# Second attention: values of two pairs of heads at once from high and low parts, and weights split inside the first attention

## What is computed

```python
q = jnp.einsum('bsm,hmd->bshd', x, W_Q) + b_Q
k = jnp.einsum('bsm,hmd->bshd', x, W_K) + b_K
v = jnp.einsum('bsm,hmd->bshd', x, W_V) + b_V
scores = jnp.einsum('bqhd,bkhd->bhqk', q, k) / jnp.sqrt(jnp.float32(D_HEAD))
scores = jnp.where(causal, scores, jnp.float32(-jnp.inf))
pattern = jax.nn.softmax(scores, axis=-1)
z = jnp.einsum('bhqk,bkhd->bqhd', pattern, v)
attn_out = jnp.einsum('bqhd,hdm->bqm', z, W_O) + b_O
```

## Time and profile before

| what | value |
|---|---|
| median of 3 runs | 1392.21 us |
| the profiled execution | 1392.85 us, of which 1390.9 us from first to last instruction |
| mean granted TensorE clock | 0.986 |
| second attention | from 539 us to the end |
| one pair there (10 groups) | 102.3 to 103.3 us for pairs 1 to 6 |

### The profile page before, as it was taken

The page is one execution under the profiler, slowest core; times in us unless marked ns, Lnnn a source line. Parts: engine busy times, 40 slices in busy tenths (PEclk is TensorE's granted clock), DMA queues, the critical chain, the costliest instruction groups (busy, mean ns, idle before and its releaser), DMA issues. The chain is left out here.

```text
span 1390.9 us, 26533 instructions
## 1 busy us (share of the span) xinstructions
PE 1304.0 (94%) x9904; PEld 688.7 (50%) x9904; DVE 1027.2 (74%) x1819; ACT 753.9 (54%) x1254; POOL 684.5 (49%) x525
## 2 busy tenths in 40 slices
PE   5889999999999987989999999999999999999897
PEld 3763222222222245555655655555555655655554
DVE  7767888888888865876766766776766776766768
ACT  5476777877777874334444444444444444443343
POOL 4101150100001010658788787777788788788671
PEclk9899999999999999999999999999999999999998
DMA  1522400000000000000000000000000000000000
GB/s 36 179 101 80 133 20 1 2 1 1 1 1 1 2 1 1 1 1 1 1 1 1 2 0 2 1 1 2 1 1 1 1 1 1 1 1 1 8 9 16
DMA packets 18172, 21.58 MB, mean 16 GB/s; under 512 B 7784, under 2 KB 15872, under 8 KB 16512
## 3 DMA queue, kind: packets, MB, share of 16 engines
q1 hardware_dynamic: 18048, 19.88, 4.4%
HBM read 14.63 MB, written 5.24 MB: 14 GB/s over the span
## 5 line engine op out<-in xcount | busy, mean ns | idle before, releaser
L1751 POOL TENSOR_TENSOR acc<-acc,prob 128x1024 f32<-128x1024 f32 (+3 forms) x250 | 493.4, 1974 | 86.4 <-ACT prob L1945 51.0
L2008 DVE TENSOR_REDUCE part_max<-psum 128x1 f32<-128x512 f32 (+3 forms) x640 | 353.9, 604 | 148.4 <-PE psum L1789 75.5
L1945 ACT ACTIVATE prob<-psum 128x1024 f32<-128x1024 f32 (+3 forms) x274 | 242.9, 897 | 287.4 <-PE psum L1840 279.5
L679 DVE TENSOR_SCALAR w<-psum 128x512 f32<-128x512 f32 x472 | 304.6, 686 | 59.3 <-PE psum L536 47.6
L630 ACT ACTIVATE w<-psum 128x512 f32<-128x512 f32 x552 | 293.9, 601 | 85.9 <-PE psum L536 85.6
L556 PE MATMUL psum<-w,v_cols 128*32 128x512 f32 x2048 | 273.7, 607 | 0.0
L1859 PE MATMUL psum<-prob,v_pair 128*64 128x512 f32 (+3 forms) x1280 | 250.2, 532 | 0.6 <-POOL prob L1719 0.6
L1837 PE MATMUL psum<-q_hi,k_hi 64*128 64x512 f32 (+3 forms) x640 | 135.5, 408 | 29.0 <-DVE part_max L2008 13.5
L1859 PEld LDWEIGHTS psum<-prob,v_pair 128*64 128x64 f32 x1280 | 87.6, 137 | 144.9 <-issue 133.8
L1784 PE MATMUL psum<-k_hi,q_hi 64*128 64x512 f32 (+3 forms) x640 | 135.5, 411 | 5.7 <-DVE part_max L2008 2.4
L1837 PE MATMUL psum<-q_lo,k_hi 64*128 64x512 f32 (+3 forms) x640 | 123.5, 366 | 0.0
(11 more groups left out here) (305 smaller groups left out, 1455.8 us busy)
## 6 DMA issues: line engine op xcount, KB each, us to landing
q_rows<-q_dram SPq DMA_DIRECT2D x12, 256.0 KB
k_rows<-k_dram SPq DMA_DIRECT2D x3, 1024.0 KB
x<-in_L_attn_x SPq DMA_DIRECT2D x4, 256.0 KB, 4.0
mask<-in_L_ffn_attention_mask SPq DMA_DIRECT2D x1, 1024.0 KB, 6.4
q_dram<-x_high SPq DMA_DIRECT2D x1, 1024.0 KB, 6.8
q_dram<-x_low SPq DMA_DIRECT2D x1, 1024.0 KB, 7.1
k_dram<-q_rows SPq DMA_DIRECT2D x1, 1024.0 KB, 9.3
k_dram<-k_rows SPq DMA_DIRECT2D x1, 1024.0 KB, 6.2
```

The lines of the kernel that those rows point to most:

```text
L679: nc.vector.tensor_scalar(w[:, s % WR, 2 * m + 1, :], pair_bank[n % RING][1], 0.0, None, ALU.max)\
L1751: nc.gpsimd.tensor_tensor(sums, sums, prob[:, s % PR, :, q0:C], ALU.add).then_inc(summed, 1)
L1945: last = nc.scalar.activation(prob[:, s % PR, :, q0:C], sh.psum[:, first:first + 2, q0:C], ACT.Exp, scale=SCALE)
L2008: free(nc.vector.tensor_reduce(part_max[:, m, i, c:c + 1], src[m][:, 0:cols], AX_X, ALU.max), unit, m)
```

## The change

Five things change.

1. A value unit now serves two pairs. It makes, for four tiles of 128 tokens, three float32r products of 256 columns each into half a bank, and takes two banks. `wv_high` and `wv_low`, the parts of W_V, are made at the start of the second attention by ACT and POOL.
2. The value units are no longer in every pair. Even pairs have one in groups 0 and 1 (the last two chunks of tokens for that pair and the next), odd pairs have one in groups 7 and 8 (the first two chunks for the next two pairs). Groups 6 and 8 of even pairs, and groups 0, 1 and 6 of odd pairs, have none. Within a group the value unit now comes ahead of mix and turn. Pair 0 keeps all four at its start.
3. ACT copies each value unit in two copies of one bank, to both pairs' tiles.
4. `w_high` and `w_low` of W_K and W_Q are no longer made in `between` (one cast on ACT, one subtraction on DVE) but in the first attention: 32 casts of 128x64 on ACT, one to a step in turns 9 to 11, and two subtractions of 128x1024 on POOL behind its last chunk.
5. The bias of the values is read by TensorE as a broadcast operand, without a copy in `prob`, and ACT does not wait for that product.

```diff
@@ -471,6 +472,8 @@
         SPARE = [s for s in range(STEPS)
                  if s % T == DIVIDE and s >= T or s in AFTER and AFTER[s][1] in DVE_FULL or s < G * T and s % T == 12]
         ON_ACT = [2 * s + 1 for s in SPARE]
+        PIECES = 2 * H
+        PIECE_AT = [s for s in range(9 * T, 12 * T) if s not in SPARE and s % T not in (LAG - 1, LAG, DIVIDE - 1)][:PIECES]
         ACTS, DVES = [], []
         for n in range(2 * STEPS):
             ACTS.append((ACTS[-1] if n else 0) + (2 if n in ON_ACT else 1))
@@ -520,6 +523,11 @@
                 join_result(nc, link, sh, c, x_done)
                 pool.wait_ge(scaled, 2 * c + 2)
                 join_normal(nc, sh, c, normed)
+                if c == NC - 2:
+                    pool.wait_ge(high_parted, PIECES)
+                    for m in range(2):
+                        nc.gpsimd.tensor_tensor(sh.w_low[:, m, :, :], sh.w_heads[:, m, :, :],
+                                                sh.w_high[:, m, :, :].bitcast(F32), ALU.subtract)
 
         @block.tensor
         def _(pe):
@@ -608,6 +616,12 @@
                     act.wait_ge(out_turned, turn)
                 nc.scalar.copy(sh.o_sb[:, :], out_bank[turn % 2]).then_inc(out_copied, 1)
 
+            def high_part(n):
+                m, h = divmod(n, H)
+                if n == 0:
+                    act.wait_ge(sh.second_loaded, SECOND)
+                nc.scalar.copy(sh.w_high[:, m, h, :], sh.w_heads[:, m, h, :]).then_inc(high_parted, 1)
+
             def copy_rows(c):
                 act.wait_ge(o_turned, c + 1)
                 if c:
@@ -631,6 +645,8 @@
                             .then_inc(act_relu, 1)
                 if kt == LAG - 1 and turn:
                     copy_out(turn - 1)
+                if s in PIECE_AT:
+                    high_part(PIECE_AT.index(s))
                 if s - COPY_O in JOIN:
                     copy_rows(JOIN[s - COPY_O])
                 if s in AFTER and AFTER[s][1] == VARIANCE + 1:
@@ -1417,8 +1432,6 @@
             deviation(1)
             gate(2, 1)
             gate(2, 2)
-            act.wait_ge(sh.second_loaded, SECOND)
-            nc.scalar.copy(sh.w_high[:, :, :, :], sh.w_heads[:, 0:2, :, :]).then_inc(w_high_done, 1)
             finish(1)
             take_xn(3)
             for f in range(F1T):
@@ -1482,9 +1495,6 @@
             join_refine(nc, link, sh, 1, at_last, scaled)
             multiply(2, 1)
             multiply(2, 2)
-            dve.wait_ge(w_high_done, 1)
-            nc.vector.tensor_tensor(sh.w_low[:, :, :, :], sh.w_heads[:, 0:2, :, :],
-                                    sh.w_high[:, :, :, :].bitcast(F32), ALU.subtract)
             take_low(3)
             for f in range(F1T):
                 multiply(3, f)
@@ -1557,16 +1568,17 @@
                     [("value", 0, 2)],
                     [("project", 0, 3), ("turn", 0, 2), ("mix", 0, 0)],
                     [("value", 0, 3), ("project", 1, 0)]]
-        WHOLE = [[("value", 0, 2)],
-                 [("value", 0, 3), ("mix", -1, 3)],
+        WHOLE = [[],
+                 [("mix", -1, 3)],
                  [("mix", 0, 0), ("turn", 0, 2)],
                  [("project", 1, 0)],
                  [("project", 1, 1)],
                  [("turn", 0, 3), ("mix", 0, 1)],
-                 [("project", 1, 2), ("value", 1, 0)],
+                 [("project", 1, 2)],
                  [("mix", 0, 2), ("turn", 1, 0)],
-                 [("value", 1, 1)],
+                 [],
                  [("project", 1, 3), ("turn", 1, 1)]]
+        VALUES = [{0: 2, 1: 3}, {7: 0, 8: 1}]
 
         def rows_phase(k):
 
@@ -1583,7 +1595,10 @@
 
             if k < len(STARTING):
                 return STARTING[k]
-            return [(kind, k // LAPS + ahead, c) for kind, ahead, c in WHOLE[k % LAPS] if k // LAPS + ahead < NP]
+            hp, at = divmod(k, LAPS)
+            first = hp + hp % 2
+            values = [("value", first, VALUES[hp % 2][at])] if at in VALUES[hp % 2] and first < NP else []
+            return values + [(kind, hp + ahead, c) for kind, ahead, c in WHOLE[at] if hp + ahead < NP]
 
         def units_of(k):
 
@@ -1593,10 +1608,9 @@
         BEFORE = [("project", 0, 0), ("project", 0, 1)] + TILES[0:TC] + [("value", 0, 0), ("turn", 0, 0), ("bias", 0, 0)]
         LAST = [("total", FINAL, None), ("mix", NP - 1, NC - 1)]
         HALVES = 2
-        TH = TC // HALVES
         UNIT = BEFORE + [u for k in range(GROUPS) for u in units_of(k)] + LAST
         AT = {u: n for n, u in enumerate(UNIT)}
-        WIDE = ("scores", "maximum", "project")
+        WIDE = ("scores", "maximum", "project", "value")
         BANKS, EARLIER, FREED = {}, {}, {}
         held, freed, place = [None] * RING, [0] * RING, 0
         for u in UNIT:
@@ -1614,13 +1628,15 @@
             return hp * NC + c
 
         wo, row_o, causal, ident_b, ones_r, own_tile = sh.wo, sh.row_o, sh.causal, sh.ident_b, sh.ones_r, sh.own_tile
+        wv_high, wv_low = (sb(name, [P, H * HD1], F32R) for name in ("wv_high", "wv_low"))
         bias = sb("bias", [P, 3, NP])
         q_hi = sb("q_hi", [P, S], F32R)
         q_lo = sb("q_lo", [P, S], F32R)
         k_hi = [sb(f"k_hi{n}", [P, S], F32R) for n in range(2)]
         k_lo = [sb(f"k_lo{n}", [P, S], F32R) for n in range(2)]
         max_rows = sb("max_rows", [P, S], F32R)
-        v_pair = [sb(f"v_pair{n}", [P, T, P]) for n in range(2)]
+        v_both = sb("v_both", [P, 2, T, P])
+        v_pair = [v_both[:, n, :, :] for n in range(2)]
         prob = sb("prob1", [P, PR, 2, C])
         acc = sb("acc", [P, 2, 2, C])
         z = sb("z", [P, 2, C])
@@ -1628,7 +1644,6 @@
         neg_max = sb("neg_max", [P, 2, 2, W])
         inv = sb("inv", [P, C])
         attn = sh.xa[:, :, 0:D]
-        bias_v = prob[:, 0, :, :].rearrange("p m c -> p (m c)").rearrange("p (n c) -> p n c", c=P)
 
         consts_set = sem("consts1_set")
         bias_turned = sem("bias_turned")
@@ -1710,6 +1725,9 @@
         @block.gpsimd
         def _(pool):
             nc.gpsimd.memset(neg_max[:, :, :, :], 0.0).then_inc(consts_set, 1)
+            pool.wait_ge(bias_done, 2)
+            nc.gpsimd.tensor_tensor(wv_low[:, :], sh.w_heads[:, 2, :, :].rearrange("p h d -> p (h d)"),
+                                    wv_high[:, :].bitcast(F32), ALU.subtract).then_inc(consts_set, 1)
 
             def hide_later(s):
                 hp, qc, kt = STEP[s]
@@ -1766,11 +1784,15 @@
 
             def value(hp, c):
                 to = room_for(("value", hp, c))
+                pe.wait_ge(consts_set, 2)
+                at = slice(hp * P, (hp + 2) * P)
                 for j in range(TC):
                     t = c * TC + j
-                    last = nc.tensor.matmul(to[0][:, j * P:(j + 1) * P], sh.xnT[:, t * P:(t + 1) * P],
-                                            sh.w_heads[:, 2, 2 * hp:2 * hp + 2, :].rearrange("p h d -> p (h d)"),
-                                            start=True, stop=True)
+                    tokens = slice(t * P, (t + 1) * P)
+                    half = to[j // TH][:, j % TH * 2 * P:(j % TH + 1) * 2 * P]
+                    nc.tensor.matmul(half, sh.x_high[:, tokens], wv_high[:, at], start=True, stop=False)
+                    nc.tensor.matmul(half, sh.x_high[:, tokens], wv_low[:, at], start=False, stop=False)
+                    last = nc.tensor.matmul(half, sh.x_low[:, tokens], wv_high[:, at], start=False, stop=True)
                 last.then_inc(unit_filled, 1)
 
             def maximum(hp, i, c):
@@ -1850,7 +1872,7 @@
                     pe.wait_ge(exp_done, s + 1)
                 if kt % TC == 0 and kt // TC == qc:
 
-                    wait_freed(pe, ("value", hp, qc))
+                    wait_freed(pe, ("value", hp - hp % 2, qc))
                 if kt == 0 and g:
 
                     pe.wait_ge(z_copied, g)
@@ -1862,9 +1884,9 @@
 
             def mix_bias():
                 to = room_for(("bias", 0, 0))
-                pe.wait_ge(bias_done, 2)
+                pe.wait_ge(bias_done, 1)
                 for n in range(NP):
-                    last = nc.tensor.matmul(to[0][:, 0:D], bias_v[:, n, :], wo[:, n, :], start=n == 0, stop=n == NP - 1)
+                    last = nc.tensor.matmul(to[0][:, 0:D], bias[:, 2, n:n + 1].to_broadcast([P, P]), wo[:, n, :], start=n == 0, stop=n == NP - 1)
                 last.then_inc(unit_filled, 1)
 
             def fill(unit):
@@ -1908,9 +1930,8 @@
             act.wait_ge(bias_turned, 1)
             nc.scalar.copy(bias[:, :, :], out_bank[:, 0:3 * NP].rearrange("p (m n) -> p m n", m=3))\
                 .then_inc(bias_done, 1)
-            nc.scalar.copy(bias_v[:, :, :], out_bank[:, 2 * NP:3 * NP].unsqueeze(2).to_broadcast([P, NP, P]))\
-                .then_inc(bias_done, 1)
-            act.wait_ge(bias_done, 2)
+            nc.scalar.copy(wv_high[:, :], sh.w_heads[:, 2, :, :].rearrange("p h d -> p (h d)")).then_inc(bias_done, 1)
+            act.wait_ge(bias_done, 1)
 
             def split_high(hp, c):
```

(7 more changed lines are left out.)

3 lines of the change are left out of this document (2 added, 1 removed).

## The result

The change made the kernel faster: 1384.3 us, the median of 4 runs (1383.88 to 1384.9), against 1392.83 of the kernel before on the same chip (4 runs, 1391.16 to 1393.51). The ratio is 0.9947, with a 95% interval of 0.9935 to 0.996; by the medians that is 8.5 us, by the ratio 7.4. On another chip, with 5 runs of the one and 11 of the other, it was 0.9954 (0.9942 to 0.9966), and the medians lay 6.9 us apart. The profiled execution after took 1383.88 us, with a span of 1381.9, 9.0 less than before.

A forecast was written before the change was run, and what follows sets the result against it. The prediction took TensorE, busy 94% of the span, as the bound, with DVE holding it after totals. Second attention -2.5, block between -0.9, and +0.2 gave -3.2 us on 1392.85, a median of 1389.0; range 1383.5 to 1393.5.

The forecast's parts named there:

- rival 1: Second attention: DVE does not hold group 7, so group 6 gives the full 1.0 us; 1383.4 us; chance 15%.
- Price of the new unit: Value units, second attention: 12 matmuls of 256 columns at 0.115 us, 1.58 a unit, 1.48 ahead of a mix.
- Rival 2: Value units: narrow matmuls paced by something other than columns (weight loads), up to 0.23 each, +22 us, 1411; chance 8%.
- Where it counts: Second attention, gains and costs group by group from removed and added value units: -2.5 us in all.
- group 6 gives 0.2 and not 1.0: Group 6, every pair but the last: removing the unit frees TensorE but not DVE, so -0.2 us, not -1.0.
- the new stop of 0.53 on `part_max`: Group 7 of seven pairs: TensorE newly stops about 0.8 us before its second scores unit.
- pairs 1 to 6: Second attention: even pairs change by -0.1 us each, odd ones by -0.2, together -0.9.
- The block between: Between the attentions: without cast and subtraction `x_low` comes earlier, TensorE's stop of 0.73 us and a hand-off go: -0.9.
- The casts in the first attention: First attention: 32 ACT casts of 0.2 to 0.27 us, covered by TensorE: 0, with +0.3 for steps where ACT is late.
- Pair 0 and pair 7: Second attention: pair 0 gets three wide units, loses those of groups 6 and 8, +0.3 us; pair 7 loses two, -1.9.
- Rival 3: Granted clock: new stops bring one or two more low-clock stretches, 1390.7 to 1392.4 us, or POOL is late, 1392; chance 25%.

The follow-up runs named there:

- run with parts alone: Changed kernel, but nothing paired: one value unit a pair at the old places, three float32r products of 128 columns a tile; 1399.27 us, ratio 1.004 to the kernel before.
- experiments with units behind totals: Changed kernel with value units moved behind totals: three of every four, 1380.04 us; pair 0's last two also, 1380.27; odd pairs' unit also in group 0 instead, 1377.88.
- the first experiment: Kernel before with only the parts of W_K and W_Q made early (new first attention and block between, old second attention); 1390.77 us, ratio 0.998.
- the run that kept it: Kernel before with only the new second attention (value units), first attention and block between as before; 1388.45 us, ratio 0.9956.
- widening alone: Changed kernel with wide value units at the new places in plain float32, without high and low parts; 1389.92 us, ratio 0.9977 to the kernel before.

## Why the prediction was right, and where its sizes were off

The forecast of 1389.0 had the direction and, for the work, the mechanisms. The measured 1384.3 lies 4.7 below it: 3.2 us were forecast and 8.5 measured. It is still inside the range, near its lower end, but that is luck, since that end came from rival 1, which the groups refute, and what brought the time there was in large part the clock.

**Price of the new unit.** Right. 0.115 was forecast for a matmul and 0.12 measured, 1.58 for the unit and 1.60 measured. Rival 2 is out. All of these matmuls load the full array, the trace shows loads of 0.19 each, the load at 772.18 runs under the matmul that began at 772.10, and the matmuls follow each other at 0.12. The Trainium skill ("TensorE: Matmul & The Clock Gate", Part 3, on packing small matmuls) says in one place that a weight load overlaps running matmuls only where the row groups differ, and in another that a load into the background weight buffer may go ahead too. By these rows the first does not hold here; the second the trace agrees with, though it does not show the buffer. The run with parts alone adds what the prediction only bounded: below 256 columns the pitch hardly falls (0.11 at 128). It is that floor which makes pairing worth while.

**Where it counts.** Right, group by group: all eight rows of the first table are within 0.2 us of the forecast and of its sign. The claim on which the forecast differed most from a count of TensorE's work was that group 6 gives 0.2 and not 1.0. It gave 0.38, and the new stop of 0.53 on `part_max` stands where it was forecast, at 0.5 and not 0.8. Rival 1 is out with it. The term was too small by 0.18, and six pairs make 1.1 of that, which is the difference between -0.9 and -1.92 for pairs 1 to 6; the misses of the other rows cancel. From `k_hi` to the second scores unit the forecast was 6.64 and 6.60 is measured, so it isn't there. It lies behind that unit, where the trace of before hides one more stall that the page does not print as idle time. Its timeline, start of group 7 of pair 2:

```profile
845.49 1.02 ACT L1945 ACTIVATE prob<-psum 128x1024 f32<-128x1024 f32 x1 [5.02 <-PE psum L1840]
...
846.21 0.41 PE L1840 MATMUL psum<-max_rows,ones_r 64*128 64x512 f32 x2
846.66 0.44 PE L1784 MATMUL psum<-k_hi,q_hi 64*128 64x384 f32 x2
```

And of the kernel after, the same place:

```profile
842.79 1.08 ACT L1972 ACTIVATE prob<-psum 128x512 f32<-128x512 f32 x2 [4.61 <-PE psum L1862]
...
844.29 0.42 PE L1862 MATMUL psum<-max_rows,ones_r 64*128 64x512 f32 x2
844.52 0.37 PE L1806 MATMUL psum<-k_hi,q_hi 64*128 64x384 f32 x2
```

From the subtracted maximum to the next maximum unit it was 0.45, and is 0.23. Before, the first scores unit came so late that its exponential ended only at 845.49 + 1.02 = 846.51, 0.15 ahead of that maximum unit; after, it has ended while TensorE still stands in the new stop. The new stop hides the old one. That ACT's exponential was what it waited for is read from the times alone. The experiments with units behind totals confirm the reading from the other side: time put into that place is free up to the stop and costs in full beyond it.

**What POOL does to DVE.** The forecast took the multiplication of z at a fixed time. In group 1 it took from 0.69 to 1.40, as shown above, and its rows there missed by 0.14 and 0.19. In the sum the two nearly cancel, so this is no part of why the total was off.

**The block between.** The stop was worth 0.97 (0.9 forecast). The other 1.67 are the clock.

**The casts in the first attention.** Forecast +0.2, measured -0.07, and 385.85 against 385.61 in the run with them alone: nothing that can be told from zero. A cast takes 0.25 us, within the 0.2 to 0.27 of the prediction, and from 318 to 394 us TensorE was busy for all 76.00, as in the earlier trace rows.

**Pair 0 and pair 7.** Pair 0 gave +0.05 for +0.3. Pair 7 gave 1.03 in group 0 and, of the 1.99 in group 1, about 0.75 in work; with +0.26 later on this is 1.5, for 1.9. Of what came later, group 4 took 0.40 more, and DVE's multiplication of z there 1.39 in place of 0.69.

**The granted clock: the step that was mis-sized.** Rival 3 took it as a loss only ("one or two more such stretches make 1390.7 to 1392.4"). The sum of work in the profiled executions is -9.0 less three clock terms, 1.67 at 534 us, 1.25 in group 1 of pair 7 and 1.26 in its groups 2 and 3: 4.2 us of clock and 4.8 of work, where 3.2 had been forecast. The rows for it stood ahead of the prediction: a clock of 0.69 at 534 us, and 4.57 against 2.84 for the same matmuls. They were used as the price of a new stretch, and never as something that the change could give back.

How much of that is owed to the change is only partly shown. Over 43 runs of the kernel before, in three groups, the mean clock had a median of 0.987 (0.982 to 0.989); over 9 runs of the kernel after it was 0.988 to 0.991. So most executions show it, not the two traces alone, though the two ranges overlap. Against each other at one clock, 0.989, before took 1391 and after 1384.5 to 1384.9, 6.3 us apart; by the traces the work is 4.8. Of the 1.5 between these two accounts, 1.0 may lie in the profiled execution of before: its pairs 1 to 6 are 1.0 shorter than those of the first experiment with the same code, since in groups 1 of pairs 2 and 6 the multiplication of z was not held. Which of the two is the usual case no run shows, and the rest stays open. What decides where a low stretch falls was not found either. The link that looked likely, the stop of 0.73 in the block between, was tried and fell: the run that kept it had no low stretch behind it in its profiled execution. And stretches come up in kernels whose code at that place is unchanged.

## What to carry to other kernels

- After a removal on the busiest engine, ask for each place which engine the next wait ends on. A value unit of 1 us gave 1.0 to 1.1 in groups where nothing else was late, 0.7 where DVE's chain became longer at the same time, and under 0.4 ahead of a stop on DVE. The reverse is worth more: work that must be done is put behind the instruction that starts the other engine's chain. The order of two units in one group was worth 1.08 us each time, and using the largest such stop twice as often took 4.8 us off; where a stop is 0.5, a unit of 1.8 there costs 1.3.
- Where narrow matmuls have a floor (here 0.11 us at 128 columns, 0.12 at 256), three products in one-pass form pay only if they are widened at the same time. Set beside the kernel with only the parts of W_K and W_Q made early, widening alone gave -0.9 us, the parts alone +8.5, the two together -6.5.
- Set the low stretches of the clock apart before reading a difference between two traces: the same two groups took 20.79, 22.03 and 23.29 us.

## What had not been expected of the hardware

- A float32r matmul of 128 columns is paced at 0.112 us, one of 256 at 0.12, one of 512 at 0.23. One instruction of a plain float32 matmul is paced at 0.11 for 128 columns and 0.216 for 256: plain float32 goes by its columns in this range and float32r does not.
- DVE's multiplication of z took 0.69 us by itself, and 1.17 to 1.40 in most groups 1, where POOL's addition was already running; it then ended 0.55 behind that. Two executions with the same code differed by 0.48 in one group, by which of the two had started first (0.02 and 0.11 us apart).
- A stretch of 3.4 us at 1.2 GHz cost 1.23 to 1.26 us where TensorE also waited, and 1.67 in the block between. In one trace such stretches came in group 1 of every other pair, and in another of the same group list not at all.
